# Two PSUM banks for the first tiles, a layer norm moved to VectorE, products of ones in TensorE's waits and new instruction orders in a two-layer attention and MoE kernel

## The chip, the cores and the metric

The kernel runs on one core of one Trainium2 chip. The metric is the device time of one execution in microseconds (us). A core has five engines that are named here as the profile names them: TensorE (PE, its weight loads PEld), VectorE (DVE), ScalarE (ACT), GpSimd (POOL) and SyncE (SP, which only starts DMAs here).

## What is computed

Four chunks (batches) of 512 tokens of width 128 run through two layers. Each step is added to x and works on a layer norm of x without scale and shift.

```python
x = x + L0_xattn(layernorm(x), ctx)     # one head, 32 keys, biases, out = (x + attended) @ Wo.T + bo
x = x + L0_ffn(layernorm(x))            # 8 experts, each token goes to the best one, exact gelu
x = x + L1_xattn(layernorm(x), ctx)     # 16 heads of width 8, 32 keys, masked
x = x + L1_ffn(layernorm(x))            # 16 experts of width 96, the best 4 in the best 2 of 4 groups, and a shared one
```

In `L0_ffn` the gates are a softmax over 8 cosine-like logits, and the chosen expert's output is scaled with its gate. In `L1_ffn` the gate is a sigmoid plus a bias, groups are ranked by the sum of their two best experts, and the block is silu(x w1) * (x w3) * gate, times w2.

## The kernel before

The program is written engine by engine. For each of four engines a string in the table `ORDER` (lines 52 to 137) lists the stages in the order in which that engine runs them, as `name:number`; each stage waits on semaphores for what it needs. So the table sets the order of the work, and the semaphores keep it right.

The names have a prefix. Stages with `a.` are attention 0 and the routing of layer 0, for chunk 0 to 3: `moments` (statistics of the layer norm), `norm` (normalise), `turn` and `unturn` (transpose and copy out of PSUM), `score`, `shift`, `exp`, `soft`, `own`, `mix`, `add` (attention and its addition to x), `norm2` and `turn2` (the second layer norm), `logit`, `pick`, `rank`, `slot`, `scatter` (choose the expert, count the place, write the token's row to its place in DRAM). Stages with `t.` are sorted tiles of 128 tokens, each with one expert: `xs` (transpose), `xc` (copy), `h` (first product), `gelu`, `y` (second product), `ys` (add the bias), `store`. Tiles 0 to 10 are group one (chunk 0, TA = 11), tiles 11 to 29 are group two (chunks 1 to 3). Without prefix: `fetch` gathers the rows back (fetch 0 to 3 chunk 0, 4 to 7 chunk 1, and so on), `combine` adds them to x; `norm2`, `turn2`, `q`, `score`, `max`, `mturn`, `scoreT`, `exp`, `zav`, `div`, `wo`, `add` are attention 1; `norm3`, `turn3`, `logit`, `sg`, `route0` to `route7`, `gturn`, `gcopy` are the last layer norm and the routing of layer 1; `g`, `u`, `e`, `silu`, `prod`, `hm`, `high`, `low`, `y` are the 52 blocks of its MoE, 13 a chunk. `w.` stages round weights into a high part (ScalarE) and a low part (GpSimd).

A layer norm runs over three engines: VectorE takes mean and variance (`statistics`, `aggregate`), GpSimd adds eps, negates the mean, takes the power -0.5 and multiplies (`rstd_of`, lines 803 to 813), ScalarE applies scale and shift in four instructions, one per 128 tokens (`normalise`, lines 611 to 619). TensorE then transposes the four pieces.

The hidden product of a tile of group one goes to bank 5, that of group two to banks 2 and 3 in turn (`h_bank`, line 526). So in group one `h` waits until the gelu of the tile ahead has read the bank (line 1438).

From `a.value` to the first `t.xs` TensorE runs one product of ones (128 x 512, bf16, result unused) ahead of each `a.` stage (lines 1591 to 1601, `FILL0 = 1`).

GpSimd issues the scatters and gathers one after another (`scatter` line 824, `fetch` line 829), each an indirect DMA of 128 rows of 512 bytes.

## Time and profile before

| | us |
|---|---|
| median of 3 runs | 311.34 (310.09 to 313.41) |
| profiled execution | 311.27 |
| span of its instructions | 309.4 |
| TensorE busy | 266.5 (86%) |
| VectorE busy | 189.3 (61%) |
| ScalarE busy | 171.1 (55%) |
| GpSimd busy | 154.0 (50%) |
| mean granted TensorE clock | 0.907 |

The span runs from the first to the last instruction; 1.9 us of the profiled execution lie around it. Busy time of TensorE is modelled, so a busy stretch isn't a stretch at peak speed. The granted clock is given as a share of 2.4 GHz; it has two levels, 1.0 (2.4 GHz) and 0.5 (1.2 GHz), and a stretch in between holds both. In the timeline a row gives the start, the duration, the engine, the line, the operation and what it writes from what; in brackets stands how long its engine sat idle before it and what ended that.

### The profile page before, as it was taken

What the parts mean: (1) busy time and instruction counts of PE and PEld (TensorE: products, weight loads), DVE (VectorE), ACT (ScalarE), POOL (GpSimd) and SP (SyncE); (2) the same over time, 40 slices, a digit from 0 to 9 for tenths busy, and PEclk for the clock granted to TensorE, in tenths of its full rate; (3) what the DMA queues carried; (4) which work ended last, traced back from release to release, by engine and by line L of the source; (5) the groups of instructions that cost most, each with busy time, mean ns of one, the idle gap of its engine ahead of it and who ended that gap; (6) DMA issues with size and microseconds to landing.
All of it is one profiled execution on the core that took longest, in us unless ns stands there. A gap on an engine that the chain in (4) does not pass through costs nothing. (4 is left out here: it accounts for less than half of the span.)

```text
span 309.4 us, 5078 instructions
## 1 busy us (share of the span) xinstructions
PE 266.5 (86%) x1543; PEld 199.4 (64%) x1543; DVE 189.3 (61%) x598; ACT 171.1 (55%) x341; POOL 154.0 (50%) x182
## 2 busy tenths in 40 slices
PE   8899979687787892286699999899999999999993
PEld 8677758575666752164357765676578877887771
DVE  5544653454254526555858789958889578755561
ACT  2834346143365681283465779489746674655541
POOL 2820557380404763778066255464347544666562
PEclk9995895589799996579689999999999999999998
DMA  7991064235663211001000000000000000000000
GB/s 232 366 397 53 12 193 118 67 87 138 179 179 101 71 38 42 17 16 54 0 0 1 2 0 1 2 0 1 36 1 0 2 35 1 0 2 34 0 2 34
DMA packets 19516, 19.44 MB, mean 63 GB/s; under 512 B 2194, under 2 KB 17154, under 8 KB 19234
## 3 DMA queue, kind: packets, MB, share of 16 engines
q1 hardware_dynamic: 13856, 14.28, 14.6%
q10 hardware_dynamic: 4610, 2.74, 2.9%
q0 software_dynamic: 1024, 2.10, 2.3%
q8 instruction: 13, 0.21, 0.3%
q14 instruction: 13, 0.11, 0.1%
HBM read 13.35 MB, written 5.77 MB: 62 GB/s over the span
## 5 line engine op out<-in xcount | busy, mean ns | idle before, releaser
L906 POOL TENSOR_TENSOR lring<-hm,hring 128x512 fp32r<-128x512 f32 (+1 forms) x52 | 66.8, 1290 | 63.0 <-ACT hring L773 62.9
L767 ACT ACTIVATE act<-bank 128x512 f32<-128x512 f32 (+1 forms) x52 | 31.0, 596 | 37.1 <-PE bank L1268 36.8
L1268 PE MATMUL bank<-xTh,gu1h 128*128 128x512 f32 (+1 forms) x104 | 45.1, 433 | 1.4 <-ACT act L767 0.7
L1234 DVE TENSOR_TENSOR act<-act,bank 128x512 f32<-128x512 f32 x48 | 32.9, 685 | 20.0 <-PE bank L1268 18.4
L1247 DVE TENSOR_TENSOR hm<-act,bank 128x512 f32<-128x512 f32 (+1 forms) x52 | 35.7, 686 | 13.1 <-PE bank L1268 9.6
L1268 PE MATMUL bank<-xTl,gu1h 128*128 128x512 f32 (+1 forms) x104 | 41.4, 398 | 0.6 <-issue 0.6
L1268 PE MATMUL bank<-xTh,gu1l 128*128 128x512 f32 (+1 forms) x104 | 41.3, 397 | 0.0
L773 ACT CAST hring<-hm 128x512 fp32r<-128x512 f32 (+1 forms) x52 | 31.5, 616 | 8.5 <-DVE hm L1247 8.0
L618 ACT ACTIVATE xn<-x,shift_of,rstd 128x128 f32<-128x128 f32 x64 | 26.4, 483 | 14.2 <-POOL shift_of L813 14.0
L706 ACT ACTIVATE hT<-bank,w 128x128 f32<-128x128 f32 x60 | 18.5, 364 | 21.5 <-PE bank L1268 19.1
L1268 PEld LDWEIGHTS bank<-xTh,gu1h 128*128 128x128 f32 (+1 forms) x104 | 19.6, 188 | 13.8 <-DVE act L1234 5.2
L1268 PE MATMUL bank<-w,hT 128*128 x120 | 22.6, 317 | 4.6 <-DVE ys L1088 3.9
L808 POOL TENSOR_SCALAR ve<-mv 128x4 f32<-128x4 f32 x16 | 3.9, 246 | 41.7 <-DVE mv L937 36.1
L1268 PE MATMUL bank<-xsT,w 128*128 128x128 f32 x120 | 21.5, 309 | 2.7 <-ACT hT L706 2.3
L1268 PEld LDWEIGHTS bank<-w,hT 128*128 128x128 f32 x120 | 18.2, 218 | 8.0 <-issue 7.9
L1268 PEld LDWEIGHTS bank<-xTh,gu1l 128*128 128x128 f32 (+1 forms) x104 | 19.7, 189 | 5.5 <-issue 0.5
L1268 PE MATMUL bank<-hring,w2h 128*128 128x512 f32 (+1 forms) x52 | 21.7, 417 | 1.6 <-POOL lring L906 1.4
L1268 PEld LDWEIGHTS bank<-xTl,gu1h 128*128 128x128 f32 (+1 forms) x104 | 19.8, 190 | 4.1 <-issue 0.8
L1268 PE MATMUL bank<-gT,sel 128*128 128x512 f32 x48 | 20.5, 427 | 2.0 <-ACT gT L761 1.7
L1268 PEld LDWEIGHTS bank<-xsT,w 128*128 128x128 f32 x120 | 18.0, 216 | 4.6 <-DVE xsT L1083 2.8
L1268 PE MATMUL bank<-hring,w2l 128*128 128x512 f32 (+1 forms) x52 | 20.5, 394 | 0.0
L1268 PE MATMUL bank<-lring,w2h 128*128 128x512 f32 (+1 forms) x52 | 20.4, 393 | 0.0
(227 smaller groups left out, 524.0 us busy)
## 6 DMA issues: line engine op xcount, KB each, us to landing
w<-in_w SPq DMA_DIRECT2D x30, 129.0 KB
wf<-in_gu SPq DMA_DIRECT2D x1, 1632.0 KB, 8.8
xs<-sorted_x SPq DMA_DIRECT2D x19, 64.0 KB
sorted_y<-ys ACTq DMA_DIRECT2D x9, 128.0 KB, 1.8
x<-in_x SPq DMA_DIRECT2D x4, 256.0 KB, 5.3
w<-in_w SPq DMA_DIRECT2D x1, 1024.0 KB, 9.7
out_x<-x SPq DMA_DIRECT2D x4, 256.0 KB, 2.0
w<-in_w SPq DMA_DIRECT2D x1, 768.0 KB, 8.4
```

The source lines that it names most:

```text
L618: nc.scalar.activation(normal(k, b)[:, j, :], x[:, b * TPB + j, :], ACT.Identity, bias=shift_of[:, ln(k, b), j:j + 1], scale=rstd[:, ln(k, ...
L706: last = nc.scalar.activation(hT0[:, t % 2, k, :], h_bank(t)[:, k * P:(k + 1) * P], ACT.Gelu, bias=b1_tile[:, t % SLOTS0, k:k + 1])
L767: nc.scalar.activation(act[0:m, n % 4, :], bank[0][0:m, :], ACT.Silu).then_inc(s.act_ready1, 1)
L773: nc.scalar.copy(hring[0:m, n % 4, :], hm[0:m, n % 4, :]).then_inc(s.hmh_ready, 1)
L808: nc.gpsimd.tensor_scalar(ve[:, own, :], mv[:, own, :, 1], EPS, None, ALU.add).then_inc(s.ln_step[k], 1)
L906: nc.gpsimd.tensor_tensor(lring[0:m, n % 4, :], hm[0:m, n % 4, :], hring[0:m, n % 4, :].bitcast(F32), ALU.subtract).then_inc(s.hml_ready, 1)
L1234: nc.vector.tensor_tensor(act[:, n % 4, :], act[:, n % 4, :], bank[1][:, :], ALU.mult).then_inc(s.prod_ready1, 1)
L1247: nc.vector.tensor_tensor(hm[0:m, n % 4, :], act[0:m, n % 4, :], bank[1 if r == SHARED[c] else 3][0:m, :], ALU.mult).then_inc(s.hm_ready1, 1)
L1268: return nc.tensor.matmul(dst, lhsT, rhs, start=start, stop=stop, skip_group_check=True)
```

## The change

1. Group one's hidden products alternate between banks 5 and 2, so `h` of tile t waits for the gelu of tile t - 2 instead of t - 1.
2. For chunk 0, all four layer norms change hands: VectorE adds eps itself, GpSimd takes the power only, and VectorE normalises with four `tensor_scalar` instructions (subtract the mean, multiply with the reciprocal deviation). Three GpSimd steps and four ScalarE steps per layer norm go away.
3. The gathers of chunks 2 and 3, which were mixed and in one row, now stand in the order of their numbers, with other steps of GpSimd between them; those of chunk 3 stand behind the first low parts of the MoE.
4. The products of ones are listed in a table `FILL`: one ahead of most `a.` stages as before (24 in place of 27), and new ones, 51 in number: 7 ahead of the last steps of attention 0 and the first tile, 4 ahead of the first tile of group two, 11 ahead of `wo:0`, 15 ahead of `turn3:0`, 2 ahead of `logit:0`, 2 ahead of `g:0`, 8 ahead of `turn2:1` and 2 ahead of `score:1`.
5. All four orders are new.

```diff
-FILL0 = 1
+FILL = {
+    "a.score:1": 1,
...
+    "a.turn2:2": 2,
+    "a.logit:2": 3,
+    "t.xs:0": 2,
+    "t.xs:11": 4,
+    "wo:0": 11,
+    "turn3:0": 15,
+    "logit:0": 2,
+    "g:0": 2,
+    "turn2:1": 8,
+    "score:1": 2,
+}
...
         def h_bank(t):
-            return bank[5 if t < TA else 2 + t % 2]
+            return bank[(5, 2)[t % 2] if t < TA else 2 + t % 2]
...
             def normalise(k, b):
                 act_e.wait_ge(s.ln_rstd[k], b + 1)
+                if b == 1 and k < 2:
+                    act_e.wait_ge(s.xn_ready[k], TPB)
...
                 pool.wait_ge(s.pool_step, 1)
+                if b == 0:
+                    nc.gpsimd.tensor_tensor(rstd[:, own, :], ve[:, own, :], mhalf[:, 0:TPB], ALU.pow).then_inc(s.ln_rstd[k], 1)
+                    return
...
                     last = nc.vector.bn_aggr(mv[:, own, j, :], st[:, own, j, :])
+                if b == 0:
+                    step(last)
+                    last = nc.vector.tensor_scalar(ve[:, own, :], mv[:, own, :, 1], EPS, None, ALU.add)
                 last.then_inc(s.ln_var[k], 1)
+
+            def normalise_first(k):
+                own = ln(k, 0)
+                v.wait_ge(s.ln_rstd[k], 1)
+                for j in range(TPB):
+                    nc.vector.tensor_scalar(normal(k, 0)[:, j, :], x[:, j, :], mv[:, own, j, 0:1], rstd[:, own, j:j + 1],
+                                            ALU.subtract, ALU.mult).then_inc(s.xn_ready[k], 1)
...
-                    elif t < TA:
-                        pe.wait_ge(s.h0_ready, t)
+                    elif t == 1:
+                        pe.wait_ge(s.aT0_ready, B)
                     else:
                         pe.wait_ge(s.h0_ready, t - 1)
...
-            filling = False
             for stage, n in order("PE"):
-                if filling and stage[:2] == "a.":
-                    for k in range(FILL0):
-                        mm(bank[5][:, :], onesb[:, :], warm_b[:, :])
                 if stage == "a.value":
                     pe.wait_ge(s.zero_ready, 1)
                     pe.wait_ge(s.a0_ready, 1)
-                    filling = True
-                elif stage == "t.xs":
-                    filling = False
+                for k in range(FILL.get(f"{stage}:{n}", 0)):
+                    mm(bank[5 if stage[:2] in ("a.", "t.") else 0 if n == 0 else 6][:, :], onesb[:, :], warm_b[:, :])
```

Of the orders one line of GpSimd's stands for all:

```diff
-        "fetch:7 rstd3:0 w.clear:0 lowx:0 rstd2:1 fetch:8 fetch:12 fetch:13 fetch:9 fetch:14 fetch:10 fetch:11 "
...
+        "rstd3:0 w.clear:0 lowx:0 rstd2:1 fetch:8 w.loww2:4 fetch:9 fetch:10 fetch:11 low:0 low:1 fetch:12 "
```

What moves is shown at three places. VectorE in attention 0, from chunk 0's attention weights (attn) on, before; x<-x,bank is the addition to x, st and mv are the statistics, m and s the scores' maximum and shift:

```order
L963 TENSOR_TENSOR attn<-s,z 128x128
L943 TENSOR_TENSOR x<-x,bank 128x512
L930 BN_STATS st<-x 128x6 x4
L937 BN_AGGR mv<-st 128x2 x4
L956 TENSOR_REDUCE m<-bank 128x4
L957 TENSOR_TENSOR s<-bank,m 128x128
L961 TENSOR_REDUCE z<-s 128x4
L962 RECIPROCAL z<-z 128x4
L963 TENSOR_TENSOR attn<-s,z 128x128
```

And now, from chunk 1's attention weights on:

```order
L1017 TENSOR_TENSOR attn<-s,z 128x128
L993 TENSOR_TENSOR x<-x,bank 128x512
L970 BN_STATS st<-x 128x6 x4
L977 BN_AGGR mv<-st 128x2 x4
L980 TENSOR_SCALAR ve<-mv 128x4
L1010 TENSOR_REDUCE m<-bank 128x4
L1011 TENSOR_TENSOR s<-bank,m 128x128
L987 TENSOR_SCALAR xn<-x,mv,rstd 128x128 x4
L1015 TENSOR_REDUCE z<-s 128x4
L1016 RECIPROCAL z<-z 128x4
L1017 TENSOR_TENSOR attn<-s,z 128x128
L993 TENSOR_TENSOR x<-x,bank 128x512
```

The addition of chunk 0 is followed by the eps step and, past chunk 2's shift, by the four normalisations; chunk 1's addition comes right behind. GpSimd between the attention of chunk 0 in layer 1 and the first blocks of the MoE, before; xn<-sorted_y,home are gathers, lring is the low part of a block:

```order
L817 TENSOR_TENSOR xTl<-xT,xTh 128x512
L808 TENSOR_SCALAR ve<-mv 128x4
L809 TENSOR_SCALAR nm<-mv 128x4
L811 TENSOR_TENSOR rstd<-ve,mhalf 128x4
L813 TENSOR_TENSOR shift_of<-nm,rstd 128x4
L829 DMA xn<-sorted_y,home 128x128 x8
L906 TENSOR_TENSOR lring<-hm,hring 96x512
```

And now:

```order
L857 TENSOR_TENSOR xTl<-xT,xTh 128x512
L848 TENSOR_SCALAR ve<-mv 128x4
L849 TENSOR_SCALAR nm<-mv 128x4
L851 TENSOR_TENSOR rstd<-ve,mhalf 128x4
L853 TENSOR_TENSOR shift_of<-nm,rstd 128x4
L869 DMA xn<-sorted_y,home 128x128
L897 TENSOR_TENSOR w2l<-ws,w2h 96x128
L869 DMA xn<-sorted_y,home 128x128 x3
L946 TENSOR_TENSOR lring<-hm,hring 96x512
L946 TENSOR_TENSOR lring<-hm,hring 128x512
L869 DMA xn<-sorted_y,home 128x128 x3
```

The eight gathers in a row are now four (one of them behind a rounding step), then three, then one, with low parts between. ScalarE at the end of the tiles, from the last store on, before; lt holds the logits of a later chunk of layer 0, sg those of layer 1, sel and gT are for the gates:

```order
L713 DMA sorted_y<-ys 128x128
L677 ACT_TABLE_LOAD
L677 ACTIVATE lt<-lt 128x32
L618 ACTIVATE xn<-x,shift_of,rstd 128x128 x4
L623 COPY xT<-bank 128x512
L630 CAST xTh<-xT 128x512
L698 CAST sel<-hm 32x1536
L753 COPY sg<-bank 128x64
L756 ACTIVATE sg<-sg 128x64
```

And now:

```order
L750 DMA sorted_y<-ys 128x128
L719 CAST gu1h<-wf 128x408
L660 COPY xT<-bank 128x512
L667 CAST xTh<-xT 128x512
L790 COPY sg<-bank 128x64
L793 ACT_TABLE_LOAD
L793 ACTIVATE sg<-sg 128x64
```

The normalisation is gone from ScalarE, and the table load now stands right ahead of the sigmoid's exponential.

## Rows read from the trace of the kernel before

**Rows 1.** The page, part 2: granted clock in 40 slices of 7.7 us, tenths.
```profile
PEclk9995895589799996579689999999999999999998
```

**Rows 2.** Windows: stretch, busy us (instructions) of PE, PEld, DVE, ACT, POOL, clock, DMA share, GB/s.
```profile
23.00:33.00 10.00, 9.89 (x43) 7.25 (x43) 4.77 (x24) 3.90 (x10) 1.12 (x3) 0.52 0.13 51
...
46.00:62.00 16.00, 12.59 (x67) 11.22 (x68) 5.76 (x29) 5.97 (x14) 8.92 (x11) 0.54 0.33 97
...
120.00:126.00 6.00, 2.05 (x8) 1.78 (x8) 3.96 (x9) 0.00 (x0) 3.92 (x4) 0.50 0.14 36
126.00:133.00 7.00, 2.92 (x10) 2.04 (x11) 2.91 (x17) 3.56 (x7) 5.53 (x7) 0.50 0.03 7
...
147.00:156.00 9.00, 6.24 (x23) 2.91 (x24) 7.03 (x21) 4.00 (x7) 0.67 (x4) 0.64 0.00 0
...
170.00:230.00 60.00, 58.02 (x353) 39.02 (x352) 49.79 (x132) 45.02 (x76) 29.50 (x31) 1.00 0.02 5
```

**Rows 3.** Timeline, TensorE in attention 0: a product of ones, the first sorted tile.
```profile
31.52 0.61 PE L1268 MATMUL bank<-warm_b,onesb 128*128 128x512 bf16 x1
...
47.11 0.38 PE L1430 MATMUL bank<-pack_a,xs 128*128 128x128 f32 x1
```

**Rows 4.** Timeline, TensorE in the tiles: h, h, first transposition of group two, y, y.
```profile
72.94 0.68 PE L1268 MATMUL bank<-xsT,w 128*128 128x128 f32 x4 [0.25 <-ACT hT L706]
...
74.43 0.68 PE L1268 MATMUL bank<-xsT,w 128*128 128x128 f32 x4 [0.34 <-ACT hT L706]
...
78.69 0.30 PE L1430 MATMUL bank<-pack_a,xs 128*128 128x128 f32 x1 [1.74 <-issue]
...
98.15 0.71 PE L1268 MATMUL bank<-w,hT 128*128 x4 [0.25 <-DVE ys L1088]
...
99.54 0.71 PE L1268 MATMUL bank<-w,hT 128*128 x4
```

**Rows 5.** Timeline, hand-over to the MoE: VectorE and TensorE.
```profile
117.78 0.29 DVE L1088 TENSOR_TENSOR ys<-bank,b 128x128 f32<-128x128 f32 x1 [1.10 <-PE bank L1268]
...
122.39 2.05 PE L1268 MATMUL bank<-pack_b,aT 128*128 128x128 f32 x8 [4.75 <-DVE aT L1142]
129.32 1.63 PE L1280 MATMUL bank<-pack_a,xn 128*128 128x128 f32 x4 [4.88 <-ACT xn L618]
...
134.34 0.20 DVE L1160 TENSOR_SCALAR sg<-sg 128x64 f32<-128x64 f32 x1 [4.99 <-ACT sg L756]
...
156.73 0.40 PE L1268 MATMUL bank<-hring,w2h 96*128 96x512 f32 x1
```

**Rows 6.** Timeline, GpSimd in attention 0 and at its last scatter.
```profile
19.78 0.24 POOL L808 TENSOR_SCALAR ve<-mv 128x4 f32<-128x4 f32 x1 [4.60 <-DVE mv L937]
...
20.41 1.04 POOL L811 TENSOR_TENSOR rstd<-ve,mhalf 128x4 f32<-128x4 f32 x1
...
35.72 1.24 POOL L824 DMA_INDIRECT first_sorted_x<-xn,slot  x1 [1.93 <-DVE slot L986]
...
65.72 0.96 POOL L824 DMA_INDIRECT sorted_x<-xn,slot  x1 [0.30 <-issue]
```

**Rows 7.** Timeline, VectorE and ScalarE in attention 0.
```profile
6.17 0.27 DVE L993 TENSOR_SCALAR bqrep<-ones,pack_a 128x128 f32<-128x128 f32 x1
...
21.75 1.65 ACT L618 ACTIVATE xn<-x,shift_of,rstd 128x128 f32<-128x128 f32 x4 [1.22 <-POOL shift_of L813]
...
48.84 1.28 ACT L706 ACT_TABLE_LOAD   x1
```

**Rows 8.** Timeline, VectorE's two long waits, and the DMA queue of instructions, 134 to 150.
```profile
58.70 0.19 DVE L970 TENSOR_REDUCE m<-bank 128x4 f32<-128x32 f32 x1 [3.68 <-remote]
...
147.47 2.48 DVE L1128 TENSOR_REDUCE mpad<-bank 128x16 f32<-128x512 f32 x4 [3.89 <-remote]
...
q8 instruction: 1, 0.02, 0.5%
```

**Rows 9.** The page, part 5: VectorE's product in a MoE block.
```profile
L1234 DVE TENSOR_TENSOR act<-act,bank 128x512 f32<-128x512 f32 x48 | 32.9, 685 | 20.0 <-PE bank L1268 18.4
```

35 lines of the change are left out of this document (33 added, 2 removed), and 150 rows, old and new, of the table ORDER.

## The prediction

> **What bounds the kernel now.** I read the clock line of the page first. TensorE's granted clock is far from full in several stretches [rows 1], and the table of windows says which: 23 to 33 us (0.52), 46 to 62 (0.54), 120 to 133 (0.50), 147 to 156 (0.64) [rows 2]. There TensorE mostly has work and does it at the lower of its two levels (1.2 against 2.4 GHz), or waits for others. From 170 us on it is busy 58.0 of 60 us at clock 1.00: the MoE of layer 1 is bound by matmuls, and no new order frees much there. The time to be had lies ahead of it.
>
> So I cut the span (309.4 us; the profiled execution took 311.27, 1.9 around it, and the median of the runs is 311.34, so both stand for the same time) by the places where one stage hands to the next. The first sorted tile is transposed at 47.11 [rows 3], the first tile of the second group at 78.69 [rows 4], the last tile leaves VectorE at 117.78 and the first y block stands at 156.73 [rows 5]. That is 47.1 us of attention 0, 31.6 of group one, 39.1 of group two, 39.0 of the hand-over to the MoE, and 152.7 of MoE.
>
> **Attention 0 (47.1 us).** The chain of chunk 0 goes VectorE, GpSimd, ScalarE: four GpSimd steps from 19.78, the power alone 1.04 us [rows 6], then ScalarE's four normalisations, 1.65 us from 21.75 to 23.40 [rows 7]. That is 3.6 us. The new one: one small VectorE step (0.24, as on GpSimd), the power 1.04, four VectorE steps on 128x128 at 0.27 (the row of bqrep, the same form with one scalar [rows 7]) = 1.1, and three hand-overs of about 0.15: 2.8 us. Saved 0.8 each time it is on the path, which is twice here: 1.6. Two scalars per row were not seen on VectorE; if they double the step, 1.1 more per chunk and the gain is gone.
> The half clock of 23 to 33 covers 9.89 us of busy time, so up to 4.9 could come back. But one 512-column product of ones per stage stood there too (at 31.52 it took 0.61 us [rows 3]) and the clock was low all the same. The new order keeps one per stage. I take 1.5 of 0 to 4.9.
> The order: VectorE now does chunk 1's addition ahead of chunk 0's pick, TensorE does mix 1 ahead of turn2 0 and only own 2 between logit 0 and rank 0. Before, the scatter of chunk 0 waited until 35.72 for its slots [rows 6]. Two steps of TensorE that stood ahead (mix 1 and the third transposition, about 2 and 1 us at half clock) go elsewhere, one (mix 2) comes in: 1.9 saved, between -1 and 3. The four scatters themselves stay at a pitch of 1.26 us (0.96 and a gap of 0.30, as the last one shows).
> Term: 1.6 + 1.5 + 1.9 = 5.0.
>
> **Group one (31.6 us).** Three things cost here. First, VectorE waits 3.68 us for logits that TensorE had long made (release named "remote", at 58.70), and it comes at the end of eight scatters in a row; the same picture stands at 147.47 (3.89 us on VectorE) at the end of eight gathers [rows 8]. The change breaks the first burst with a rounding step (w2 low, piece 0) and rstd2, and the second into 4, 3 and 1. If the bursts make the stall, it goes. I take half: 1.8 of 0 to 3.7.
> Behind that row the Trainium skill has another rule ("Advanced Engine Details and Errata", ISA Cache): an engine's instructions come in lines of 256, two at a time. An instruction packet does move in the window of the second stall [rows 8]. By that rule the stall goes with the count of instructions and not with the bursts; it would only be shifted, and these 1.8 and the 2.5 below were 0. No row tells the two apart: it is the first rival below.
> Second, the half clock: 12.59 us busy at 0.54 in 46 to 62 [rows 2]; full, this is about 5.8 less. The seven products ahead of turn2 2, logit 2 and the first tile bridge the register load where it fell. Products in the tile loop itself there are none. I take 3.0 of 0 to 5.8.
> Third, the tiles. In the kernel before, each hidden product waits for the gelu of the tile ahead, since both use bank 5: 72.94 to 74.43 is 1.49 us a tile. With two banks the next limit is the chain of y and its addition: 98.15 to 99.54, 1.39 us, in group two, which has two banks already [rows 4]. So the title's first edit is worth 0.1 x 6 steady tiles = 0.6. The register load of group two moves ahead of y 9: of the 1.74 us that the first tile waits I take 1.0, since that tile's data may then be late.
> Against it: the exponentials of chunk 2 now stand between gelu 1 and gelu 2, two table loads of 1.28 [rows 7] and 0.2: 2.8 us in ScalarE's queue. Behind them stand w2 piece 0 and, through it, GpSimd's low part and seven scatters, the last of which stood at 65.72 [rows 6]. I take 1.4 of 0 to 2.8.
> Term: 1.8 + 3.0 + 0.6 + 1.0 - 1.4 = 5.0.
>
> **Group two (39.1 us).** Nineteen tiles at 1.39 are 26.4; the rest is chunk 0's attention and a fall of the clock near 80 us (the 7 in the clock line [rows 1]). Four products are added (512 columns at 2.4 GHz, 0.21 each, 0.9 in all), VectorE takes over a normalisation (1.1) from ScalarE off the path. Saved 1.5, between -2 and 4.
>
> **Hand-over (39.0 us).** At 117.78 the last addition; wo waits 4.75 us for the reciprocal (122.39), turn3 4.88 us for the normalised chunk (129.32) [rows 5], all at half clock. In 120 to 133 TensorE is busy 2.05 + 2.92 us [rows 2], so a full clock gives 2.5. The eleven products ahead of wo need 11 x 0.21 = 2.3 us, the fifteen ahead of turn3 3.2, inside the waits (turn3's shrinks to about 3.9). VectorE's normalisation gives 0.8, the two small gain steps ahead of the division go elsewhere, 0.4 (a small VectorE step is 0.20 [rows 5]). Against it: chunk 1's combine stands behind the normalisation, but it also waited for its gathers before, so I count nothing. Chunk 2's exponentials used to load the table early; now it loads at the sigmoid: 1.3 on the path to routing, which began at 134.34 [rows 5]. Routing now runs without hm 0 and prod 1 in between (products of 128x512, 0.69 us each [rows 9]): 1.3 back. The stall at 147.47: 2.5 of 0 to 3.9, as its burst is truly cut. The half clock of 147 to 156 was its echo: 1.0. Sum 0.4 + 0.8 + 2.5 - 1.3 + 1.3 + 2.5 + 1.0 = 7.2. What is late next: turn2 1 now stands ahead of u 0, and waits for GpSimd, which clears, rounds and takes a root first; for that I take off 1.7. Term 5.5, between 1 and 9.
> A rule that speaks against the VectorE steps: the Trainium skill ("SBUF — State Buffer", Who interferes with whom) says that a tensor_scalar may take both ports and then shuts GpSimd out for its length. No row of this trace shows it; by that rule 1.1 us per chunk would be added where GpSimd has work, at most 2 in all.
>
> **MoE (152.7 us).** TensorE-bound. One block's g (three products of 512 columns, 0.6 us at 2.4 GHz) is no longer done before the first y; chunks 2 and 3 arrive later but are used some 20 us later still. I take 1.0 lost, between -2 and 4.
>
> **Sum.** 5.0 + 5.0 + 1.5 + 5.5 - 1.0 = 16.0; 311.3 - 16.0 = 295.3, say 295.
>
> **The rivals.**
> 1. Clock and stalls stay; only order and engines help. For it: one product per stage did not hold the clock before, and the stalls may hang on instruction counts. Then the clock terms (1.5, 3.0, half of group two, 2.5, 1.0) and the stalls (1.8, 2.5) fall: these are 13.1 of the 16.0, and 2.9 remain. The discount of 1.7 in the hand-over is then not due either, as there the wait stays the old one. 311.3 - 2.9 - 1.7 = 306.7, say 306.
> 2. Everything arrives: clock full from 23 us on, both stalls gone. The upper ends of attention 0 (8) and group one (9), 3, 8, less 1: 27, so 284. Against it: such sums seldom come in whole, as every freed wait has a second one behind it.
> 3. Nothing to measure: the scatter chain on GpSimd (twelve at 1.26 with a rounding in between) sets group two as before and the hand-over waits for GpSimd. 310.
> 4. Slower. Place: the hand-over. If the clock is low when the last tile ends, the products of ones take 512 columns at 1.2 GHz, 0.43 each: fifteen are 6.4 us in a wait of 3.9 (2.5 over), the four around logit and g 1.7 with 0.8 of wait (0.9 over), eight ahead of turn2 1 are 3.4 ahead of u 0, two ahead of score 0.9. With the table load: 2.5 + 0.9 + 3.4 + 0.9 + 1.3 = 9.0, less the 1.2 of the shorter chain and about 3 from the earlier stages: 316. It decides once the overrun is above what the first two stages give. Against it: eleven products come first and raise the share of work.
>
> **How the numbers follow.** Forecast (289 to 301) 0.50; rival 1 0.22; rival 2 0.12; rival 3 0.08; rival 4 0.08. About 1% is what a measurement of this kernel can tell from no change. Faster: 0.50 + 0.12 + 0.20 of rival 1 = 0.82; same 0.02 + 0.08 = 0.10; slower 0.08. The range leaves out the lower half of rival 2, half of rival 3 and rival 4: 285 to 308.
>
> **What would show it.** Clock line without the fives at slices 3, 6, 7 and 15 to 17; first tile near 42; first tile of group two near 69; last tile's addition near 106; first y near 140; no wait named "remote" over 3 us. I am wrong if the clock falls in the same stages, if the ones' rows last 0.6 us in the hand-over, if turn3 waits for TensorE's own products, or if the MoE has idle time that it did not have.

## The result, and the profile after

The changed kernel took 312.98 us (median of 12 runs, 309.92 to 315.56) beside 309.94 (12 runs, 307.55 to 313.41) of the kernel before on the same chip: ratio 1.0094, 95% interval 1.0048 to 1.014. It is slower by 0.9%; forecast were 295. Its profiled execution took 315.44 us, span 313.6, and so lies above its median, as that of the kernel before does (311.27).

The same two kernels stand 2.7% apart on another chip (ratio 1.0266, 1.0192 to 1.034), where the kernel before takes 296.8. (The ratios leave out executions over 1.5% above the fastest of the same kernel; on the 296 chips four to five of ten of those of the kernel before are such, and with them the two medians there, 302.7 and 296.8, are 2.0% apart.) So two kinds of chip appear below, called 310 and 296 by what the kernel before takes there (310 to 311 us, and 296 to 301). Ratios are always taken on one chip; stages are compared within a kind.

Part 2 of the page of the changed kernel, the clock in 40 slices of 7.8 us (answers to [rows 1]):
```profile
PEclk9669985576998999979799999999999999999998
```
The low digits of the hand-over (6 and 5 in slices 15 and 16, counted from 0) are gone, with a seven left on either side of slice 18. The fives of group one are not, and there is a new fall at slices 1 and 2, from 8 to 24 us.

The cuts used in the prediction, in the changed kernel's timeline: first sorted tile, first tile of group two, last tile's addition, first y of the MoE (answer to [rows 3 to 5]):
```profile
49.25 0.42 PE L1488 MATMUL bank<-pack_a,xs 128*128 128x128 f32 x1
...
83.41 0.27 PE L1488 MATMUL bank<-pack_a,xs 128*128 128x128 f32 x1
...
124.29 0.29 DVE L1142 TENSOR_TENSOR ys<-bank,b 128x128 f32<-128x128 f32 x1 [1.10 <-PE bank L1326]
...
159.31 0.39 PE L1326 MATMUL bank<-hring,w2h 96*128 96x512 f32 x1
```
By these rows attention 0 lasts 49.3 us (before 47.1), group one 34.2 (31.6), group two 40.9 (39.1), the hand-over 35.0 (38.9), the MoE 154.3 (152.7): 2.1 + 2.6 + 1.8 - 3.9 + 1.6 = 4.2 us, the difference of the spans. Only the hand-over, and the MoE with its small loss, went the way that was forecast.

What VectorE's normalisation costs, at its first use and at its last, with GpSimd's two memsets beside the last:
```profile
7.54 1.08 DVE L987 TENSOR_SCALAR xn<-x,mv,rstd 128x128 f32<-128x128 f32 x4
...
133.09 3.70 DVE L987 TENSOR_SCALAR xn<-x,mv,rstd 128x128 f32<-128x128 f32 x4 [1.17 <-POOL rstd L846]
...
133.02 1.79 POOL L914 MEMSET gT<- 128x2048 f32 x1
134.76 1.37 POOL L915 MEMSET sel<- 128x1536 f32 x1
...
136.27 1.00 PE L1338 MATMUL bank<-pack_a,xn 128*128 128x128 f32 x4 [3.44 <-DVE xn L987]
```
The same four steps on the same shapes take 1.08 and 3.70 us. The estimate of 0.27 for one step was right (two scalars do not double it); the last use starts with the memsets and ends shortly after they do. The second use, at 26.04, stands beside a GpSimd step of 1.50 us and takes 1.59.

The waits named remote are not gone, they stand elsewhere. In the changed kernel:
```profile
41.11 0.58 ACT L705 COPY aT<-bank 32x512 f32<-32x512 f32 x1 [2.82 <-remote]
...
67.55 0.29 DVE L1137 COPY xsT<-bank 128x128 f32<-128x128 f32 x1 [2.98 <-remote]
...
91.94 0.29 DVE L1137 COPY xsT<-bank 128x128 f32<-128x128 f32 x1 [3.33 <-remote]
```
The first is in attention 0, the second in group one like that of 58.70 before, the third in group two. That of 147.47 us before [rows 8] has none in its place in the hand-over: it was 3.89 us, and the hand-over is 3.9 us shorter.

### The profile page after: what moved, and what is told of

Same layout as the page of the kernel before. It is cut to its first block and busy times, and to the rows that moved or that the text cites. A ratio compares the mean times of both kernels' runs of the same rounds, so it can differ in the third digit from the quotient of the medians.

```text
span 313.6 us, 5157 instructions
## 1 busy us (share of the span) xinstructions
PE 275.9 (88%) x1584; PEld 205.3 (65%) x1591; DVE 196.9 (63%) x618; ACT 165.6 (53%) x325; POOL 151.6 (48%) x170
## 5 line engine op out<-in xcount | busy, mean ns | idle before, releaser
L1326 PE MATMUL bank<-xTh,gu1h 128*128 128x512 f32 (+1 forms) x104 | 44.4, 427 | 2.0 <-DVE act L1288 1.8
L743 ACT ACTIVATE hT<-bank,w 128x128 f32<-128x128 f32 x60 | 18.5, 366 | 31.6 <-PE bank L1326 24.5
L1326 PE MATMUL bank<-w,hT 128*128 x120 | 24.0, 331 | 5.1 <-DVE ys L1142 2.4
L1326 PEld LDWEIGHTS bank<-w,hT 128*128 128x128 f32 x120 | 19.2, 226 | 10.0 <-issue 9.6
L655 ACT ACTIVATE xn<-x,shift_of,rstd 128x128 f32<-128x128 f32 x48 | 19.9, 486 | 7.0 <-POOL shift_of L853 6.8
L1326 PE MATMUL bank<-xsT,w 128*128 128x128 f32 x120 | 23.1, 332 | 0.5 <-DVE xsT L1137 0.5
L1326 PE MATMUL bank<-warm_b,onesb 128*128 128x512 bf16 x68 | 22.1, 419 | 1.6 <-issue 1.4
L1142 DVE TENSOR_TENSOR ys<-bank,b 128x128 f32<-128x128 f32 x30 | 8.7, 290 | 23.4 <-PE bank L1326 21.6
L1137 DVE COPY xsT<-bank 128x128 f32<-128x128 f32 x30 | 8.7, 289 | 23.2 <-PE bank L1488 15.2
L1326 PEld LDWEIGHTS bank<-xTh,gu1l 128*128 128x128 f32 (+1 forms) x104 | 19.6, 189 | 4.9
L660 ACT COPY xT<-bank 128x512 f32<-128x512 f32 x16 | 9.4, 587 | 23.3 <-PE bank L1338 21.7
```

What stands on the lines that cost most here:

```text
L655: nc.scalar.activation(normal(k, b)[:, j, :], x[:, b * TPB + j, :], ACT.Identity, bias=shift_of[:, ln(k, b), j:j + 1], scale=rstd[:, ln(k, ...
L660: nc.scalar.copy(xT[:, xT_slot(k, b), :], bank[n][:, :]).then_inc(s.xT_ready[k], 1)
L743: last = nc.scalar.activation(hT0[:, t % 2, k, :], h_bank(t)[:, k * P:(k + 1) * P], ACT.Gelu, bias=b1_tile[:, t % SLOTS0, k:k + 1])
L1137: nc.vector.tensor_copy(xsT[:, t % 2, :], xs_bank(t)[:, 0:P]).then_inc(s.xsT_ready, 1)
L1142: nc.vector.tensor_tensor(ys[:, y_slot(t), :], y_bank(t)[:, 0:C], b2_0[:, bass.ds(own_expert[t], 1), :].rearrange("p o c -> p (o c)"), ALU ...
L1326: return nc.tensor.matmul(dst, lhsT, rhs, start=start, stop=stop, skip_group_check=True)
```

## The experiments

Eighteen kernels were timed, the two of the change on both kinds of chip. All cuts, in us, one profile each; the last column is the ratio to the kernel before with its interval.

| kernel | chip | first tile | group 1 | group 2 | hand-over | MoE | ratio |
|---|---|---|---|---|---|---|---|
| before | 310 | 47.1 | 31.6 | 39.1 | 38.9 | 152.7 | |
| after | 310 | 49.3 | 34.2 | 40.9 | 35.0 | 154.3 | 1.0094 (1.0048 to 1.014) |
| exp_late | 310 | 45.2 | 33.9 | 40.8 | 34.9 | 154.1 | 1.0143 (1.005 to 1.0235) |
| regs_late | 310 | 46.3 | 34.4 | 40.4 | 34.9 | 154.3 | 1.0045 (0.9995 to 1.0096) |
| old_tiles | 310 | 49.6 | 28.9 | 39.6 | 35.0 | 154.1 | 0.9921 (0.9882 to 0.9959) |
| mixed | 310 | 46.5 | 32.0 | 39.0 | 38.8 | 152.9 | 0.9981 (0.993 to 1.0033) |
| y_first | 310 | 46.8 | 35.8 | 38.9 | 33.8 | 154.3 | 1.0049 (0.9998 to 1.01) |
| before_split2 | 310 | 48.1 | 31.2 | 40.3 | 38.3 | 152.7 | 1.0017 (0.995 to 1.0083) |
| before_again | 296 | 45.5 | 23.8 | 38.4 | 32.2 | 152.6 | 1.0013 (0.9975 to 1.0051) |
| after_again | 296 | 45.0 | 31.3 | 37.5 | 33.2 | 154.3 | 1.0266 (1.0192 to 1.034) |
| clear_later | 296 | 46.6 | 28.3 | 37.5 | 34.1 | 154.3 | 1.0297 (1.023 to 1.0364) |
| early_fill | 296 | 46.2 | 29.3 | 37.5 | 34.9 | 154.3 | 1.0285 (1.0212 to 1.0357) |
| old_orders | 296 | 47.7 | 24.9 | 39.7 | 33.7 | 152.6 | 1.0169 (1.0097 to 1.024) |
| old_start | 296 | 47.4 | 26.9 | 37.6 | 33.6 | 154.3 | 1.0213 (1.0161 to 1.0265) |
| fills_only | 296 | 50.0 | 25.2 | 38.4 | 32.2 | 152.5 | 1.0051 (0.9998 to 1.0105) |
| norm_only | 296 | 43.1 | 24.1 | 39.8 | 33.6 | 152.7 | 0.9996 (0.9945 to 1.0046) |
| before_split | 296 | 46.9 | 24.5 | 38.2 | 34.8 | 152.6 | 1.0088 (1.0039 to 1.0137) |
| norm3_scalar | 296 | 46.7 | 29.0 | 37.5 | 32.0 | 154.6 | 1.0177 (1.011 to 1.0245) |
| gelu_first | 296 | 45.4 | 29.4 | 38.6 | 35.4 | 154.2 | 1.037 (1.0291 to 1.0449) |
| best2 | 296 | 47.0 | 25.3 | 38.8 | 33.4 | 156.3 | 1.0125 (1.0048 to 1.0202) |

One warning on this table: the first tile comes anywhere from 45.0 to 49.6 us in kernels with the new order of attention 0 and from 43.1 to 50.0 with the old one (45.5 to 48.1 where nothing that runs in attention 0 was touched). TensorE's clock falls in another place in each profile; whether that is all of the scatter was not shown. A stage must differ by more than that, or in every profile, before it says something.

### Both kernels again

> The kernel before, unedited, for its stages on this chip: the runs of the kernel before took 296.4 us beside the experiments so far and 309.9 beside the changed kernel's first runs, so chips differ by 4%. Theory A, the difference is the two waits named remote (3.68 us at 58.70, 3.89 at 147.47) and the clock: the profile shows neither wait, and first sorted tile, first tile of group two, last tile and first y stand some 0, 4, 5 and 11 us sooner than 47.1, 78.7, 117.8, 156.7. Rival B, the waits belong to the kernel's bursts of scatters and gathers and stay; then only the clock differs. Times 292 to 302.

> The changed kernel, unedited, beside its variants. From the variants (302.3 with the clearing later, whose normalisation took 1.1 in place of 3.7 us; 302.8 with six products more): 303 to 305, which is 2 to 3% over the kernel before on such a chip. Theory A, on a chip without remote waits the change loses more than the 0.9% first measured, since the stall that it avoided at 147 was no part of the kernel: ratio 1.020 to 1.030. Rival B: the ratio stays at 1.009.

Theory A holds in both as to the waits: on the 296 chip no wait named remote stands anywhere in either kernel. The kernel before gains more by it than the text said: first tile of group two, last tile and first y stand 9.4, 10.0 and 16.8 us sooner, not 4, 5 and 11, and its two waits are 7.6 us of the 16.8; the rest was not traced. The hand-over of the kernel before takes 32.2 us there, not 38.9, and that of the changed one 33.2, not 35.0. Without the wait the change has nothing to save in this stage and loses 0.9. The clock of the whole span, kernel before and changed, in 40 slices (7.3 and 7.5 us) as in [rows 1]:
```profile
PEclk9899975998999996599999999999999999999999
```
```profile
PEclk9999977857999999899999999999999999999999
```
The first kernel's fall of 23 to 33 us and the second's of 8 to 24 us are both gone, each in an unchanged program. Group one is the large loss: 23.8 against 31.3. TensorE's groups by shape from first tile to first tile of group two, kernel before (busy, mean ns, idle before):
```profile
L1268 PE MATMUL bank<-xsT,w 128*128 128x128 f32 x44 | 8.0, 311 | 0.4 <-DVE xsT L1083 0.4
L1268 PE MATMUL bank<-w,hT 128*128 x44 | 7.6, 295 | 1.6 <-DVE ys L1088 1.0
L1430 PE MATMUL bank<-pack_a,xs 128*128 128x128 f32 x11 | 3.6, 327 | 0.1
```
and changed:
```profile
L1326 PE MATMUL bank<-w,hT 128*128 x44 | 10.0, 366 | 2.9 <-issue 1.9 <-DVE ys L1142 0.9
L1326 PE MATMUL bank<-xsT,w 128*128 128x128 f32 x44 | 9.6, 364 | 0.8 <-DVE xsT L1137 0.7
L1488 PE MATMUL bank<-pack_a,xs 128*128 128x128 f32 x12 | 4.1, 344 | 2.0 <-DVE xsT L1137 2.0
```
The same 88 products of the tiles last 4.0 us more (19.6 beside 15.6), and TensorE is idle ahead of these rows 5.7 us in place of 2.1. The longer products go with a lower clock; the window of 62 to 70 us, kernel before and changed:
```profile
62.00:70.00 8.00, 5.10 (x31) 3.76 (x30) 3.02 (x11) 2.40 (x7) 0.81 (x1) 1.00 0.64 177
```
```profile
62.00:70.00 8.00, 6.56 (x31) 6.13 (x31) 3.01 (x11) 3.77 (x11) 1.72 (x2) 0.62 0.51 143
```
Half of the loss stands ahead of the first sum: it comes 8.9 us behind the first tile in place of 5.2, so 3.7 of the 7.4 us are lost before it and as much behind it.

The MoE's 1.7 us are TensorE's idle time: from the first y to the end it is busy 145.1 us before and 145.2 changed, and idle 7.5 and 9.1. The waits for VectorE grew, from 1.3 us to 4.1, most of it for the products of the blocks (act, 0.5 and 1.8) and for attention 1's maxima (mpad, 0 and 1.4).

### Parts of the change alone

fills_only: the kernel before with a table FILL in place of FILL0, which keeps its 27 products and adds the 51 new ones.

> The kernel before with the table of products of ones alone: one per stage of attention 0 as it was, and two, three, two, four more ahead of the first tiles, eleven ahead of wo, fifteen ahead of the last norm's transposition, two ahead of logits, two ahead of g 0, eight ahead of the second chunk's turn2, two ahead of its scores. Theory A, they lie in TensorE's waits and hold the clock: hand-over 2 us shorter, time 1 to 2 us less than before. Rival B, they are on the path where the wait is shorter than they are (12 of them stand ahead of g 0, turn2 1 and scores 1, 2.5 us at full clock, where the kernel before has TensorE busy), and the clock was the same without: 1.5 to 3 us more than before.

Nearer to rival B, though the 0.5% is at the edge of the interval, and the windows say why. From the last tile on, kernel before (busy us, then the clock as third value from the right):
```profile
107.74:113.74 6.00, 1.40 (x6) 1.43 (x7) 4.68 (x7) 1.51 (x2) 2.73 (x3) 0.80 0.18 47
113.74:119.74 6.00, 1.17 (x6) 0.67 (x4) 4.33 (x21) 1.07 (x3) 4.08 (x7) 0.50 0.08 22
119.74:125.74 6.00, 5.20 (x17) 3.46 (x17) 1.37 (x7) 5.14 (x9) 5.02 (x7) 0.57 0.00 0
```
and with the products of ones:
```profile
113.62:119.62 6.00, 3.62 (x20) 1.98 (x20) 4.84 (x8) 1.51 (x2) 2.74 (x3) 1.00 0.16 42
119.62:125.62 6.00, 4.23 (x19) 1.83 (x18) 4.17 (x21) 1.65 (x4) 4.99 (x8) 1.00 0.09 23
125.62:131.62 6.00, 4.50 (x22) 2.46 (x19) 2.56 (x11) 5.74 (x10) 5.07 (x7) 1.00 0.00 0
```
They do hold the clock, all through the hand-over, and the hand-over lasts 32.2 us with them and without. The layer's addition comes 5.9 us behind the last tile in place of 6.8, and that 0.9 is gone at the first y. TensorE is idle 12.8 us of the hand-over without them and 7.2 with them, waiting for VectorE and ScalarE, so its own speed isn't what sets the end of the stage.

norm_only: the kernel before with normalise_first, old orders, old products, one bank.

> The kernel before with VectorE's normalisation of chunk 0 alone (four norms), the orders, the products of ones and the bank as before. Theory A, VectorE gains 0.8 us at each of the first three norms but is shut out by GpSimd's memsets at the last one (3.7 us for its four steps in four of five profiles, 1.1 in the one where the memsets stand later): net 0 to 2 us more than before. Rival B, it is the useful part of the change: 1.5 us less than before.

The lower end of theory A: no difference that the interval would show. The last norm's steps take 3.70 us again, as in all eleven profiles in which VectorE does them beside the memsets, and hand-over with MoE is 186.2 us beside 184.9.

clear_later, in GpSimd's table:
```
-rstd3:0 w.clear:0 lowx:0 rstd2:1
+rstd3:0 lowx:0 w.clear:0 rstd2:1
```

> The changed kernel, with one edit: GpSimd clears the gate table and the selector (the two memsets, 1.79 and 1.37 us) after the low half of chunk 0's input instead of before it. Theory A, GpSimd's memsets keep VectorE out: in the changed kernel the four steps that normalise chunk 0 of the last norm took 3.70 us from 133.09, beside 1.08 for the same four at 7.54, and the memsets stood at 133.02 and 134.76. Then the four steps take 1.1 us, the transposition of that chunk (3.44 us of wait before) comes 2.6 us sooner, and the first y block stands about 2 us sooner (157.3 in place of 159.31); time 310.5 to 311.5 beside 313.0. Rival B, the steps are slow there for another reason (two pointers for scalars and data fresh from the addition): they stay at 3.70 us and the time at 313. Rival C: the steps are quick, but the memsets now hold the root of chunk 1 or VectorE's routing, and the first y stays at 159.

Its VectorE and GpSimd:
```profile
121.15 1.12 DVE L990 TENSOR_SCALAR xn<-x,mv,rstd 128x128 f32<-128x128 f32 x4 [1.17 <-POOL rstd L849]
...
126.76 2.05 DVE L1217 TENSOR_SCALAR sg<-sg 128x64 f32<-128x64 f32 x1 [2.12 <-ACT sg L796]
...
125.64 1.80 POOL L917 MEMSET gT<- 128x2048 f32 x1
127.39 1.38 POOL L918 MEMSET sel<- 128x1536 f32 x1
```
A is right on the mechanism and C on the time. The steps are back at 1.12 us; the tensor_scalar of the routing, 0.19 us in after_again, now takes 2.05 and ends with the second memset; and the root of chunk 1 is late, so its transposition waits 3.02 us. The Trainium skill ("SBUF — State Buffer", Who interferes with whom) says of the port pair that the two engines share that the one that issues first keeps it for its whole instruction, and the other stands still. The trace agrees, in the direction that the prediction had left out: the memset comes first, and VectorE's step ends only after it (3.70 and 2.05 us, against 1.12 and 0.19).

norm3_scalar: in the changed kernel, `norm3:0` goes from VectorE's table back to ScalarE's.

> The changed kernel, with chunk 0 of the last norm normalised by ScalarE as in the kernel before; the memsets stay where they are. VectorE's four steps take 3.7 us there beside the memsets; ScalarE's path costs the two more small GpSimd steps (0.7), and 1.65 for its four: 2.4 beside 3.7 to 3.8. Theory A, the transposition of that chunk comes 1.3 us sooner and the first y follows: hand-over 32 in place of 33.2, ratio 0.004 below the changed kernel's (1.0094 where the kernel before takes 310, 1.0266 where it takes 296). Rival B, behind it the second chunk's turn sets the end, as in the kernel with the later clearing: no change in the ratio. Rival C: the memsets then collide with routing: 0.003 more.

Theory A: the hand-over is 32.0 us in place of 33.2, and of 33.6 to 35.4 in three other kernels with the changed order there (early_fill, old_start, gelu_first). (The ratio is lower by 0.009, but it was measured on another chip.)

early_fill:
```
+    "a.turn:0": 2, "a.score:0": 1, "a.route:0": 1, "a.turn:1": 1, "a.value:0": 1,
```
Two waits of TensorE that these need come with them.

> The changed kernel with six more 512-column products of ones early in attention 0: two ahead of the first transposition, one each ahead of the first scores, the routing weights, the second transposition and the value product. Theory A, the clock fell at 11 us (0.77, 0.50, 0.50, 0.52 in the four stretches of 3 us from 9, beside 1.00 in each before) because TensorE stood idle near 7.3 and had only short steps then: with the products it stays at full, V is ready about 1.3 us sooner, and the first addition moves from 22.70 to 18 to 20 us; the slots of chunk 0 come sooner by the part that VectorE does not hold, so the first sorted tile stands at 46 to 48 beside 49.25, and the time at 310 to 312. Rival B, the order is what costs there (scores of chunk 1 and the value product ahead of chunk 0's weights): the clock stays up but the addition comes no sooner than 21.5. Rival C, the clock falls all the same, and the six products cost 1 to 2 us: 314.

It tells nothing of them: on the 296 chips the clock was 1.00 from 9 to 21 us with the six products and, in after_again, without them. So the fall at slice 1 of the first profile does not come in every execution of the kernel.

### Where in the orders

old_orders: the four tables of the kernel before, the rest changed.

> The changed kernel with the four order tables of the kernel before; VectorE's new normalisation steps stand in them where ScalarE's stood in sense (behind the moments, behind chunk 0's addition and the like). Two banks, the products of ones, and the waits stay as changed. Theory A, the new orders are what lost the time and the rest is worth something (two banks 0.6, the norm 0.8 to 1.6, the clock in the hand-over up to 2.5): 305 to 309. Rival B, the orders were the useful part and the rest costs: 314 to 318. Rival C, nothing of either can be told: 310 to 313.

old_start: the old tables up to the first tile only.

> The changed kernel, with the orders of the kernel before up to the first sorted tile (on TensorE to the third second-norm transposition, on VectorE to chunk 2's slots, on ScalarE to chunk 3's weights, on GpSimd to the eighth scatter), and the new orders behind it. Theory A, the new order of attention 0 puts the scores of chunk 1 and the value product ahead of chunk 0's weights and so loses 5 us at the first addition and 2.1 at the first sorted tile: with the old order the first sorted tile is back at 47 or sooner and the time at 310 to 311. Rival B, all that follows makes up or eats that: 313 with the first sorted tile at 47. Rival C, the new start is the better one and the loss comes later: 314 to 316.

Both texts spoke of a chip where the kernel before takes 310, and this was a 296; the ratios must do. Against the changed kernel's 1.0266 (another 296 chip) the old orders are at 1.0169: the new ones cost 1% as a whole, about the size of the intervals, as the first half of theory A has it. By the table they lose 3 to 6 us in group one and 1.7 in the MoE, and win 1 to 2 in group two. The second half fails: the rest of the change is worth nothing, it costs 1.7% over the kernel before. The products of ones alone (0.5%) and the norm alone (0.0%) do not add up to that; the second bank alone was not run, and where the other 1.2% lie, with intervals of 0.5 to 0.7% either way, stays open. The old start is nearest to its rival B: it wins nothing in attention 0 (47.4), and its ratio is that of the changed kernel within the intervals, though group one behind it is 26.9.

old_tiles: the changed kernel with the old order of group one on all four engines (the exponentials of chunks 1 and 2 go behind the tiles with it).
```
-t.xs:0 t.xs:1 t.h:0 a.turn2:3 a.rank:2 t.h:1 t.xs:2 a.logit:3 t.xs:3 t.h:2 t.xs:4 t.h:3 t.y:0
+t.xs:0 t.h:0 t.xs:1 a.turn2:3 a.rank:2 t.xs:2 t.h:1 t.y:0 t.xs:3 a.logit:3 t.xs:4 b.kv:2 t.h:2 t.y:1
```

> The changed kernel with the orders of the kernel before in group one alone, on all engines (from the first sorted tile to the last of the first group); attention 0 ahead of it and all behind it as changed, and the exponentials of chunks 1 and 2 go late. Theory A, the new order of group one is the main loss of the change: group one 24 to 26 us in place of 31.3, ratio to before 1.005 to 1.010. Rival B, group one is late because attention 0 hands it its rows and slots in another order (the stall for chunk 2's slots, 4.50 us at 49.63, comes with the prefix): 28 to 30 us, ratio 1.018. Rival C: the loss only moves on to the second group: 1.025.

Theory A: group one takes 28.9 us in place of 34.2, and the ratio of 0.9921 lies 0.017 below the changed kernel's, as the text said for the other kind of chip. Here the kernel is faster than both. The remote wait in its group one is 2.45 us beside 2.98, so it is not that wait that made the 5.3. GpSimd's and ScalarE's tables change in group one too, so this run does not say by itself which engine's order it is. Its first tile and first y sum:
```profile
49.57 0.42 PE L1491 MATMUL bank<-pack_a,xs 128*128 128x128 f32 x1
...
55.27 0.29 DVE L1145 TENSOR_TENSOR ys<-bank,b 128x128 f32<-128x128 f32 x1 [1.32 <-PE bank L1329]
```
5.7 us; in exp_late and regs_late, run beside it, this is 10.1 and 8.9. On the 296 chips it is 4.5 to 5.5 in six kernels with the old order of group one and 7.8 to 10.1 in six with the new. On the 310 chips the kernel before has 7.4 and the changed one 10.1.

exp_late moves `a.pexp:2` behind the tiles.

> The changed kernel with one pair moved back: the exponentials of chunk 2's gate (ScalarE, two changes of its function table of 1.28 us) leave their place between the activations of the second and third tile and go ahead of those of chunk 3, behind the tiles; the small VectorE step that uses them goes with them. In the changed kernel group one lasts 31.3 us (45.00 to 76.27) beside 23.9 in the kernel before (45.45 to 69.30) on the same chip. Theory A, the 2.8 us of ScalarE stop the tile loop while it has only two tiles under way, and the rounding behind it holds GpSimd's scatters: group one 28 to 29, time 300 to 301 beside 302.7, ratio to before 1.018. Rival B, they lie beside the wait for tiles and slots: group one stays at 31, ratio 1.027. Rival C: group one is bound by the last scatter, which comes 1.1 us sooner at most.

Rival B: group one 33.9 us. The two table changes cost the stage nothing that shows.

regs_late moves TensorE's `t.regs:1` from ahead of y 9 to ahead of the first tile of group two.

> The changed kernel with TensorE's load of the second group's registers moved back behind the last products of the first group, where the kernel before has it. In the changed kernel TensorE stands still 1.88 us for it at 68.88 to 71.03, and then does the ninth product, the value keys' turn and the tenth at half clock until 75. Theory A: the load stops a full queue and lowers the clock, and the second group waits for its rows anyway: group one 29 to 30 in place of 31.3, ratio to before 1.021. Rival B, it only moves: the first tile of the second group then waits for it, 31.3 again, ratio 1.027. Rival C, it was right where it was: 32 to 33.

Group one did not shrink (34.4), as rival B says. The load stalls TensorE at either place, 1.22 us ahead of the first tile of group two here and 1.83 us ahead of y 9 in the changed kernel.

gelu_first:
```
 ACT  -a.unturn2:3 a.pexp:1 t.gelu:0 t.gelu:1 a.pexp:2
      +t.gelu:0 a.unturn2:3 t.gelu:1            (a.pexp:1, 2 ahead of a.pexp:3)
 PE   t.regs:1 as in regs_late
```

> The changed kernel with four moves toward the old order of group one, the order of its tiles on TensorE and VectorE left as changed: the first tile's activation ahead of the copy of chunk 3's transposition, the exponentials of chunks 1 and 2 behind the tiles (with their VectorE steps), and TensorE's register load behind the group's last product. Theory A, these are the cost: in the changed kernel the first y product of the group stands at 52.64 beside 49.88 in the kernel before, and the register load takes another 1.9: group one 4 us shorter, ratio 0.012 to 0.015 below the changed kernel's. Rival B, the tile order itself and the half clock that its waits bring are the cost: the first y comes sooner but the last does not; ratio at most 0.005 lower.

Rival B, and worse than it: group one 29.4 us, no less than the 28.3 to 29.3 of three kernels that left it as it was (31.3 in after_again). The first activation starts at 47.68 (after_again 50.00), but y 0 stands in TensorE's queue behind the hidden product of the fourth tile all the same. Its hand-over is 2.2 us longer; why was not followed up. What is left of old_tiles' edit is the tile order of TensorE and VectorE, and the places of the roundings on ScalarE and GpSimd, which were not tried alone.

y_first, TensorE (VectorE's additions likewise):
```
-t.xs:2 a.logit:3 t.xs:3 t.h:2 t.xs:4 t.h:3 t.y:0 a.rank:3 t.xs:5 t.y:1
+t.xs:2 a.logit:3 t.y:0 t.xs:3 t.h:2 t.y:1 t.xs:4 t.h:3 a.rank:3 t.xs:5
```

> The changed kernel with two TensorE steps and two VectorE steps of group one moved: the second product of the first tile ahead of the fourth tile's transposition, that of the second tile ahead of the fifth's (both stood behind the hidden product of the fourth tile), and their additions accordingly. Theory A, the new order lets four tiles' first halves go ahead of the first y, and each later y waits in line: the first addition then stands 6 us behind the first sorted tile in place of 9 to 10, group one is 2 to 3 us shorter (26.5 to 28 in place of 28.3 to 31.3 where the kernel before takes 296; 31 to 32 in place of 34.2 where it takes 310), ratio 0.006 to 0.010 below the changed kernel's. Rival B, the tiles are bound by the rows and slots that come for them: the first addition is sooner but the last is not, ratio as the changed kernel's. Rival C, the hidden products then wait for the activation, as in the kernel before, and the gain is under 1 us.

Not settled, and no support for theory A. The first sum comes 8.0 us behind the first tile, not 6, and group one takes 35.8, not 31 to 32. TensorE stands still 4.00 us in it beside a remote wait, but 2.56 in the changed kernel at the same place, so without the surplus it would still be 34. The ratio of 1.0049 is below the changed kernel's 1.0094 by about the size of the intervals. So that the late y 0 is what makes the new order slow is not shown; that the order as a whole is, old_tiles shows.

### The waits named remote

before_split, GpSimd of the kernel before:
```
-a.scatter:7 a.scatter:8 ... a.scatter:15 w.mask:0
+a.scatter:7 w.mask:0 a.scatter:8 ... a.scatter:15
-fetch:8 fetch:12 fetch:13 fetch:9 fetch:14 fetch:10 fetch:11 fetch:15 low:0
+fetch:8 fetch:9 fetch:10 fetch:11 low:0 fetch:12 fetch:13 fetch:14 fetch:15
```

> The kernel before with two bursts of GpSimd's indirect DMAs broken: the mask's rounding (1.7 us) between the fourth and fifth of eight scatters, and the first low half of the MoE between the fourth and fifth of eight gathers. Theory A, the waits named remote come with bursts, on some chips: each ended 0.2 to 1.7 us behind the end of a burst of 4 to 8 in all seven profiles of the slower kind of chip (58.7 behind 57.2, 147.5 behind 145.8 in the kernel before) and none stood in the others. If this chip is of the slower kind, the wait at 147 goes and the one near 58 is at most 2 us, ratio to before 0.985 to 0.992; if it is of the quicker kind, no wait in either and 0.998 to 1.005. Rival B, the waits go with TensorE's instruction loads (an instruction packet stood in 56:57 and 145:146): on the slower kind they stay, 3.7 and 3.9 us, ratio 1.000.

(The profiles with such waits were six by then, not seven.) It met a 296 chip, without them, and was slower by 0.9% where theory A allowed 0.5, with 2.6 us more in the hand-over. `low:0` now runs in the middle of VectorE's routing, which had the gathers beside it before (first row: before_again):
```profile
130.51 0.23 DVE L1201 TENSOR_TENSOR route<-route 128x64 f32<-128x64 f32 x1
```
```profile
132.43 1.55 DVE L1204 TENSOR_TENSOR route<-route 128x64 f32<-128x64 f32 x1
...
132.60 1.29 POOL L909 TENSOR_TENSOR lring<-hm,hring 96x512 fp32r<-96x512 f32 x1
```
The same small step takes 1.55 us in place of 0.23 and ends 0.1 us behind `low:0`, and the gate is 1.3 us later. This looks like the memsets' case once more, with another GpSimd step (in before_split2 a step of the routing takes 1.20 us beside the rounding that was put among its gathers); the other 1.3 us of the hand-over were not traced.

before_split2: the same break among the scatters, and `w.loww2:3` and `w.loww2:4` among the eight gathers.

> The kernel before with both bursts broken by work that GpSimd has in any case: the mask between the eighth and ninth scatter of the run (1.7 us), and two low parts of w2 (1.0 and 0.5 us) among the eight gathers. Theory A, remote waits need a burst of four or more: on the slower kind of chip the wait at 147 (3.9 us) goes, that near 58 stays at 2 to 4 since the scatters still run by fours and more, ratio 0.985 to 0.992; on the quicker kind there is no wait to remove: 0.998 to 1.005. Rival B: the waits stay at 3.7 and 3.9 us on the slower kind; ratio 1.000.

Rival B by the ratio; the waits on VectorE are 1.21 and 3.12 us, shorter than 3.7 and 3.9 but there. GpSimd's last steps and the second wait, on both engines:
```profile
145.03 0.95 POOL L832 DMA_INDIRECT xn<-sorted_y,home  x1 [0.30 <-issue]
146.00 0.46 POOL L860 TENSOR_TENSOR w2l<-ws,w2h 96x128 fp32r<-96x128 f32 x1
146.62 0.97 POOL L832 DMA_INDIRECT xn<-sorted_y,home  x1 [0.16 <-issue]
147.89 0.95 POOL L832 DMA_INDIRECT xn<-sorted_y,home  x1 [0.30 <-issue]
...
149.67 1.89 DVE L1131 TENSOR_REDUCE mpad<-bank 128x16 f32<-128x512 f32 x3 [3.12 <-remote]
149.73 0.57 ACT L764 CAST gT<-bank 32x512 fp32r<-32x512 f32 x1 [5.62 <-remote]
```
Gaps of 1.2 and 0.6 us do not end it; the wait ends 0.8 us behind the last indirect DMA, not behind the first burst. Nor does rival B's reason stand: in mixed the wait stood from 54.4 to 58.0, and the DMA queues of 54 to 58 hold no instruction packet:
```profile
q0 software_dynamic: 117, 0.23, 16.6%
q1 hardware_dynamic: 11, 0.00, 0.4%
```
What holds in the eight profiles of 310 chips: where VectorE or ScalarE waits for TensorE while GpSimd issues indirect DMAs one behind another, the release can be late, and comes up to 1.7 us behind the last of them (once, at 62.97 here, 1.6 us ahead of it). What it is, and why the 296 chips have none of it, stays open.

### Mixtures

mixed: old orders, with the new order of group two; VectorE for the first three norms.

> A mixture meant to beat both: orders of the kernel before, except the second group's, which are the changed kernel's (37.5 us beside 38.4 to 39.8 with the old ones, in the profiles on this kind of chip); VectorE normalises chunk 0 of the first three norms, ScalarE that of the last, as before, since GpSimd's memsets keep VectorE out there; products of ones and bank as before. Theory A, the stages add up: attention 0 no longer than 45.5, group one 24, second group 37.5, hand-over 32.2, MoE 152.6: ratio 0.990 to 0.995. Rival B, what the second group gains by the new order was taken from the hand-over (deferred loads and weights): 0.998 to 1.003. Rival C: the seams of the two orders cost: 1.005 or more.

Rival B or no difference: group two 39.0, as before.

best2: old_tiles, with norm3 on ScalarE and the old order of the MoE from the second y block on.

> The changed kernel with the old order in group one and, from the second y block on, in the MoE, and chunk 0 of the last norm normalised by ScalarE. Kept of the change are its attention 0, its second group, its hand-over (broken bursts) and the products of ones. Theory A, the stages add: 0.992 (old order in group one alone, on the slower kind of chip) less 1.7 us of MoE and 1.3 of the hand-over: ratio 0.980 to 0.985 on a chip where the kernel before takes 310, and 1.000 to 1.005 where it takes 296. Rival B, the MoE's 1.7 us come with the later chunks and not with the order: 0.988 on the former.

It met a 296 chip and is 1.2% slower than the kernel before, where theory A said 0 to 0.5%; group one is right (25.3), the MoE 156.3, more than with either whole order; why was not traced. No version was found that beats the kernel before on 296 chips; old_tiles, which does on the 310 chip, was not run there.

## Why the prediction was wrong

The sum of 16.0 us saved became 4.2 lost in the profiles. Its two terms of 5.0 for attention 0 and group one are what failed first.

**Attention 0 (-5.0).** It was +2.1 in the first profile and -0.5 between the two profiles of a 296 chip. The norm's step is quicker, as forecast: chunk 0 is normalised at 8.62, before at 9.93. It does not reach the first tile: over eleven profiles with the new start that stands at 46.7 us in the mean, over nine with the old at 46.9. Where it is lost was not traced. The step that failed was to read the half clock of 23 to 33 us as part of the kernel: in before_again the same stretch has a clock of 1.00. The 1.9 for the order did not show either.

**Group one (-5.0).** This is the main error. I took the second bank as 0.1 a tile and put the order of the tiles that came with it at nothing. It costs 5.3 us by old_tiles on the 310 chip and, on the 296 chips, by six kernels with the old order (23.8 to 25.3) against five with the new (28.3 to 31.3), with 26.9 where the new order follows the old start. Which move in it costs is not shown. The new order puts y 0 behind the hidden products of four tiles, and the first sum comes 3.7 us later (296 chip), but y_first, which puts y 0 back, did not shorten the stage. Of the other parts, the register load (-1.0) and the exponentials (+1.4) measured about 0 in the stage, and the 3.0 of clock came with the opposite sign: the new order leaves TensorE idle 5.7 us in place of 2.1 ahead of the tiles' products, and the clock from 62 to 70 us is 0.62 in place of 1.00. The bank is worth nothing at full clock: norm_only has one and old_orders two, and the additions behind y follow each other at 1.39 us in both.

**Group two (-1.5).** -0.9 on the 296 chip, as forecast; on the 310 chip a remote wait of 3.3 us moved into it.

**Hand-over (-5.5).** -3.9 on the 310 chip, and +0.9 on the 296 chip. The 2.5 for the stall was the one term that came in, at 3.9, and by luck: its reason, that cutting the burst ends the wait, fails in before_split2 (3.12 us with the burst cut), and the changed kernel has 6.3 us of such waits on VectorE in place of 7.6, in other stages, and one of 2.8 on ScalarE besides. The 2.5 for the clock was 0 by fills_only: the clock rose, the stage did not shorten. The 0.8 for VectorE's norm was a loss: 1.3 us of hand-over and MoE by norm_only, 1.2 of hand-over by norm3_scalar. I had weighed the shared port, but asked only what GpSimd loses and not what VectorE does; the memsets that now stand beside it I had read in the order and given no price.

**MoE (+1.0).** +1.6, with every kernel that has the whole new MoE order at 154.1 to 154.6 and all with the old at 152.5 to 152.9. The sign is right and the size inside its range; the loss is TensorE waiting for VectorE and not the one block that I counted.

**The rivals.** Rival 4 had the sign and nothing else: the products of ones did not overrun (the fifteen took 3.40 us, and TensorE stood idle another 3.44 behind them). Rival 1 was nearest in mechanism (clock and stalls stay) and missed the order's cost. The range of 285 to 308 left out the slow side because each stage ahead of the MoE was summed to a saving; what the new tile order makes wait had no term.

## What to carry to other kernels

When a change adds a buffer and a new order, cost the order by itself, with a kernel that has the one without the other. A stage's clock is worth something only if TensorE sets the stage's end: full clock for 32 us saved nothing. Before an operation goes to VectorE, or one of GpSimd's moves, look what the other engine runs at that moment. And a wait that moves with the chip and not with the kernel is no term of a sum.

## What was not expected of the hardware

- GpSimd's memset (1.80 and 1.38 us) shuts VectorE's tensor_scalar out: 3.70 in place of 1.08 us for four, 2.05 in place of 0.19 for one. Beside a GpSimd tensor_tensor of 1.29 us a VectorE tensor_tensor took 1.55 in place of 0.23 (one profile each).
- The same program takes 310 us on some chips and 296 on others, with waits named remote of 1 to 6.9 us on the former and none on the latter. A change was 0.9% slower on one and 2.7% on the other.
- TensorE's clock falls at other places in each profile of the same early program: from 23 to 33 us it was 0.52 in one profile of the kernel before and 1.00 in the other.
